# A two-layer triangle kernel: masks on the finished operands, and centring moved to VectorE

## The reference

```python
# layer 0 ("z")
z_norm = layer_norm(z)                         # over the 64 channels
a = (z_norm @ W_ap + b_ap) * sigmoid(z_norm @ W_ag + b_ag) * mask
b = (z_norm @ W_bp + b_bp) * sigmoid(z_norm @ W_bg + b_bg) * mask
z = z + (einsum('bikc,bkjc->bijc', a, b) @ W_z + b_z)
# layer 1 ("x")
x = layernorm(z)
left, right = sigmoid(x @ left1) * (x @ left2), sigmoid(x @ right1) * (x @ right2)
p = layernorm(einsum('nsre,nkre->nske', left, right))
out = z + einsum('nrse,ez->nsrz', p, out_w) * sigmoid(x @ gate)
```

## Time and profile before

| | us |
|---|---|
| median of 3 runs (lowest, highest) | 1227.56 (1223.94, 1231.35) |
| profiled execution | 1227.42 |
| its span | 1225.6 |
| PE, DVE, ACT, POOL busy | 900.5, 807.3, 583.7, 690.2 |
| POOL's pow x192 | 377.3 |
| POOL's mask of the gate x128 | 182.6 |

### The profile page before, as it was taken

One profiled execution on the slowest core, in us unless ns is written; L12 is line 12 of the kernel. 1 busy time (PEld: TensorE's weight loads), 2 busy tenths in 40 slices (PEclk: granted clock), 3 DMA queues, 4 the chain that ended last, 5 costly groups with the idle time before them and its releaser, 6 DMA issues.

```text
span 1225.6 us, 26377 instructions
## 1 busy us (share of the span) xinstructions
PE 900.5 (73%) x9820; PEld 849.1 (69%) x9820; DVE 807.3 (66%) x1883; ACT 583.7 (48%) x834; POOL 690.2 (56%) x441
## 2 busy tenths in 40 slices
PE   1546555467867689676967888888998999956965
PEld 1445454467867579665955888888898999946854
DVE  4888898945658851888167347662597299089097
ACT  1566666653935443455334445553454355333333
POOL 2576777766658851888045213331486188178097
PEclk9876667787988989999988899999999999989989
DMA  2334357776876733665766425676486288866156
GB/s 71 110 106 130 110 146 233 225 237 237 293 218 200 211 103 100 190 196 175 245 210 182 137 78 175 204 260 243 127 305 205 81 293 285 260 219 224 44 190 206
DMA packets 173238, 228.72 MB, mean 187 GB/s; under 512 B 11064, under 2 KB 109624, under 8 KB 171064
## 3 DMA queue, kind: packets, MB, share of 16 engines
q1 hardware_dynamic: 173112, 227.04, 59.4%
HBM read 134.73 MB, written 92.27 MB: 185 GB/s over the span
## 4 chain that ended last, share of the span: by engine, by line
PE 28%; DVE 26%; POOL 19%; issue 17%; ACT 4%; DMA 3%; SPq 2%; DVEq 0%; POOLq 0%; ACTq 0%
PE bank L918 18%; POOL rstd L511 13%; DVE stats L762 7%; DVE xc L795 6%; POOL sig L504 5%; DVE lhs L745 3%; PE ps_w L948 3%; PE bank L902 2%; DVE xc L787 2%; PE bank L903 2%; DVE var L770 2%; POOL xc L523 2%; DMA chunk<-xt 1%; DVE rhs L745 1%; PE ps_x L959 1%
## 5 line engine op out<-in xcount | busy, mean ns | idle before, releaser
L511 POOL TENSOR_TENSOR rstd<-var,minus_half 128x8 f32<-128x8 f32 x192 | 377.3, 1966 | 375.1 <-DVE var L770 375.0
L918 PE MATMUL bank<-rhs,lhs 128*128 128x128 f32 x2048 | 245.6, 283 | 15.5 <-DVE rhs L745 9.0
L504 POOL TENSOR_TENSOR sig<-sig,masks 128x512 f32<-128x512 f32 x128 | 182.6, 1433 | 128.4 <-ACT sig L569 127.5
L569 ACT ACTIVATE sig<-bank 128x512 f32<-128x512 f32 x256 | 153.1, 598 | 212.0 <-PE bank L903 202.0
L918 PEld LDWEIGHTS bank<-rhs,lhs 128*128 128x128 f32 x2048 | 241.0, 198 | 16.5 <-DVE rhs L745 9.5
L959 PE MATMUL ps_x<-ident_b,split 128*128 128x128 bf16 x1024 | 101.1, 257 | 142.9 <-DVE split L802 142.8
L795 DVE TENSOR_TENSOR xc<-xc,rstd 128x504 f32<-128x504 f32 (+1 forms) x192 | 161.1, 839 | 62.3 <-POOL xc L523 35.0
L902 PE MATMUL bank<-w_lhs,chunk 128*128 128x128 bf16 x1024 | 157.1, 242 | 51.7 <-DVE lhs L745 37.9
L902 PE MATMUL bank<-w_rhs,chunk 128*128 128x128 bf16 x1024 | 158.7, 245 | 40.4 <-DVE rhs L745 29.6
L959 PEld LDWEIGHTS ps_x<-ident_b,split 128*128 128x128 bf16 x1024 | 78.0, 116 | 158.5 <-DVE split L802 134.6
L948 PE MATMUL ps_w<-w_out,opair 128*128 128x128 f32 x1024 | 152.0, 296 | 39.1 <-DVE split L809 35.4
(11 more groups left out here) (83 smaller groups left out, 1348.7 us busy)
## 6 DMA issues: line engine op xcount, KB each, us to landing
xt<-xt SPq DMA_DIRECT2D x96, 512.0 KB, 4.4
chunk<-xt SPq DMA_DIRECT2D x80, 512.0 KB, 4.4
xin<-in_x_dram SPq DMA_DIRECT2D x128, 256.0 KB, 3.0
x<-xin SPq DMA_DIRECT2D x64, 256.0 KB, 3.7
xin<-x SPq DMA_DIRECT2D x64, 256.0 KB, 3.9
out_dram<-xin SPq DMA_DIRECT2D x64, 256.0 KB, 3.2
spill<-lhs SPq DMA_DIRECT2D x8, 1024.0 KB, 6.4
chunk<-xcol SPq DMA_DIRECT2D x16, 512.0 KB, 4.0
```

The lines of the kernel that those rows point to most:

```text
L504: g.tensor_tensor(sig[:, s], sig[:, s], table[:, other, first:first + COLS].unsqueeze(1).broadcast_to([P, C, COLS]), ALU.mult).then_inc(ma ...
L511: g.tensor_tensor(rstd[:, m % 2], var[:, m % 2], minus_half[:, :], ALU.pow).then_inc(rooted, 1)
L569: a.activation(sig[:, s], v[:, 0:C, :], ACT.Sigmoid).then_inc(gated, 1)
L918: last = mm(bank[:, n], operand["lhs"][:, kh, c, :], operand["rhs"][:, kh, c, :], start=kh == 0, stop=kh == HALVES - 1)
```

## The change

There are four edits, made together.

1. **Masks.** `mask_gate` goes: `make` waits for `gates` directly. Instead, finished operands are multiplied in place. POOL does 48 operations of 4 channels (128x512): one a tick from tick 22, two a tick from tick 54 (`mask_operand`). DVE does 24 of 8 channels (`mask_group`), eight at the start of each of the contractions 0 (128x1024), 1 and 2 (128x2048). PE waits for all 48 before contraction 0, and for each group of DVE's before that group. SP's first spills wait for POOL's masks, the next for DVE's.
2. **Centring.** DVE does all of it, except every other step of 52 to 63. Before, POOL also had every other step of the third `x` pass, all of the fourth, and every other one of the first two `p` passes.
3. **Order in a tick.** The first pass's halves run 5 ticks behind their step (53 ticks then), and a single half counts as a "second" half, whose gate and make come in the next tick. `z` steps are centred in their own tick, and `high` comes one tick earlier. In `x` steps `normalise`, `low`, `turn_x`, `xt_out` and the store come one tick later.
4. **Order on DVE**: `variance` directly behind `statistics`; `scale` ahead of `centre`.

```diff
-    lag = 6
-    for t in range(54):
+    lag = 5
+    for t in range(53):
         tick(t if t < 52 else None, [t - lag] if t >= lag else [])
+def first_half(t):
+    return halves_at(t)[0] if len(halves_at(t)) == 2 else None
+def second_half(t):
+    return halves_at(t)[-1] if halves_at(t) else None
+POOL_MASKS = 3 * C // 4
+MASK_FIRST, MASK_TWO = 22, 54
+def pool_masks_at(t):
+    if MASK_FIRST <= t < MASK_TWO:
+        return [t - MASK_FIRST]
+    if MASK_TWO <= t < MASK_TWO + C // 8:
+        return [2 * C // 4 + 2 * (t - MASK_TWO), 2 * C // 4 + 2 * (t - MASK_TWO) + 1]
+    return []
 def centre_on_pool(m):
-    kind = step(m)[0]
-    quadrant = m // STEPS
-    if kind == "z":
-        return m >= 52 and m % 2 == 0
-    if kind == "x":
-        return quadrant == 7 or (quadrant == 6 and m % 2 == 0)
-    return quadrant < 10 and m % 2 == 0
+    return SIG_STEPS[0] <= m < SIG_STEPS[1] and m % 2 == 0
+SIG_STEPS = (52, 64)
...
             def spill(layer, kh, part):
-                sp.wait_ge(made, after(2 * ((NEEDS[0] if layer == 0 else NEEDS[4])
-                                            - (0 if kh else CHUNKS // (2 if layer == 0 else 1))) - 1))
+                if layer == 0:
+                    if kh == 0:
+                        sp.wait_ge(masked_p, 2 * C // 4 + C // 16 * (part + 1))
+                    else:
+                        sp.wait_ge(masked_v, 2 * (part + 1))
...
+            def mask_operand(n):
+                kh, c = n // (C // 4) % 2, 4 * (n % (C // 4))
+                op, table = ("rhs", mask_kj) if n < 2 * C // 4 else ("lhs", mask_ki)
+                if c == 0:
+                    pool.wait_ge(made, after(CHUNKS * (n // (C // 4) + 1) - 1))
+                part = operand[op][:, kh, c:c + 4, :]
+                g.tensor_tensor(part, part, table[:, kh, 0:P].unsqueeze(1).broadcast_to([P, 4, P]),
+                                ALU.mult).then_inc(masked_p, 1)
...
+            def mask_group(q, group):
+                op, low_kh, high_kh = VECTOR_MASKS[q]
+                table, half = (mask_ki, P * (q == 1)) if op == "lhs" else (mask_kj, P)
+                dve.wait_ge(made, after(2 * NEEDS[q] - 1))
+                part = operand[op][:, low_kh:high_kh, CG * group:CG * (group + 1), :]
+                v.tensor_tensor(part, part, table[:, low_kh:high_kh, half:half + P].unsqueeze(2).broadcast_to(
+                    [P, high_kh - low_kh, CG, P]), ALU.mult).then_inc(masked_v, 1)
...
             def contract(q, u):
...
                 if part == 0:
+                    if q == 0:
+                        pe.wait_ge(masked_p, POOL_MASKS)
+                    if q in VECTOR_MASKS:
+                        pe.wait_ge(masked_v, GROUPS_C * q + u // 2 + 1)
...
         @block.scalar
...
             for t in range(T_END):
-                before, now = halves_at(t - 1), halves_at(t)
-                if len(before) == 2:
-                    gates(before[1])
+                if second_half(t - 1) is not None:
+                    gates(second_half(t - 1))
...
+                s = step_at(t - 1)
+                if s is not None and s < X_BASE:
+                    high(s)
                 s = step_at(t - 2)
-                if s is not None and s < P_BASE:
-                    high(s)
...
+                if first_half(t) is not None:
+                    gates(first_half(t))
...
         @block.vector
...
+                if unit and second_half(t - 1) is not None:
+                    make(second_half(t - 1))
+                if unit and unit[0] in VECTOR_MASKS and unit[1] < GROUPS_C:
+                    mask_group(unit[0], unit[1])
+                for s in (due, begin):
+                    if s is not None:
+                        statistics(s)
+                        variance(s)
+                if not unit and second_half(t - 1) is not None:
+                    make(second_half(t - 1))
...
```

More of the change, by code:

```diff
@@ L494, in _ @@
                             base=0, pattern=[[-1, P]], channel_multiplier=1).then_inc(idents, 1)
[L496 to L501, removed]
-                    pool.wait_ge(ready, 1)
[L503 to L506, removed]
+            def mask_operand(n):
+                kh, c = n // (C // 4) % 2, 4 * (n % (C // 4))
+                op, table = ("rhs", mask_kj) if n < 2 * C // 4 else ("lhs", mask_ki)
+                if n == 0:
+                    pool.wait_ge(ready, 1)
+                if c == 0:
[3 more added lines that the diff above has]
+                                ALU.mult).then_inc(masked_p, 1)
             def root(m):
@@ L549, in _ @@
                     add_residual(s)
-                if now and now[0] < 8 * CHUNKS:
-                    mask_gate(now[0])
+                for n in pool_masks_at(t):
+                    mask_operand(n)
         @block.scalar
@@ L817, in _ @@
             for t in range(T_END):
-                before, now = halves_at(t - 1), halves_at(t)
                 start, ago = step_at(t), step_at(t - 1)
-                if ago is not None and X_BASE <= ago < P_BASE:
-                    statistics(ago)
+                unit = TICKS[t][2]
+                due = ago if ago is not None and X_BASE <= ago < P_BASE else None
                 if start is not None and not X_BASE <= start < P_BASE:
-                    statistics(start)
-                if len(before) == 2:
-                    make(before[1])
@@ L826, in _ @@
[L826 to L831 removed]
+                    begin = start
+                else:
+                    begin = None
+                if unit and second_half(t - 1) is not None:
+                    make(second_half(t - 1))
@@ new lines, in _ @@
+                if unit and unit[0] in VECTOR_MASKS and unit[1] < GROUPS_C:
[6 more added lines that the diff above has]
+                    make(second_half(t - 1))
+                s = step_at(t - 3)
+                if s is not None and X_BASE <= s < P_BASE:
+                    low(s)
@@ L842, in _ @@
-                if now:
-                    make(now[0])
-                if ago is not None and centre_on_pool(ago):
-                    normalise(ago)
+                if first_half(t) is not None:
+                    make(first_half(t))
                 if ago is not None and ago >= P_BASE and ago % 2 == 0:
@@ L976, in _ @@
             for t in range(T_END):
-                now = halves_at(t)
-                start, s2 = step_at(t), step_at(t - 2)
+                start = step_at(t)
+                due = start if start is not None and X_BASE <= start < P_BASE else None
+                late = step_at(t - 2) if step_at(t - 2) is not None and step_at(t - 2) >= P_BASE else None
                 unit = TICKS[t][2]
-                first = bool(now) and t > 0 and TICKS[t - 1][2] is not None
+                first = first_half(t) is not None and t > 0 and TICKS[t - 1][2] is not None
                 if unit:
```

114 lines of the change are left out of this document (59 added, 55 removed).

## The result

The changed kernel took **1269.64 us** (median of 4 runs, 1266.82 to 1272.16); the kernel before 1225.89 beside it (1223.94 to 1231.35). The ratio is 1.0349 [1.0306, 1.0392]: slower by 3.5%. The prediction was 1259 and slower. The profiled execution took 1270.9, its span is 1269.1, its mean granted clock 0.88. In the experiments one execution of `e6_masks_ahead` (2714.88 us) and one of `e7_centring_alone` (1272.33 us) was disturbed; the ratios leave it out, the medians count it.

What follows compares the result with a forecast made beforehand. No engine bound the whole span; a loop through DVE, ACT and POOL set the first pass. Terms 47 + 13 - 3 + 9 + 5 - 19 - 17 - 1 - 8 + 6 = +32 on 1227.4 gave 1259 us, range 1226 to 1288.

Steps and rivals of the forecast that it cites:

- First pass: First pass: ticks lengthen through a closed wait loop, and POOL's masks hold low from tick 22; +60 us together.
- The ring: First pass: normalise, high, two copies, gate, make, low, centre wait in turn each tick; 5.50 us instead of 4.5, +47.
- The mask's hold: First pass from tick 22: POOL's operand mask delays DVE's low by 0.45 on 30 ticks; +13 us (0 to 32).
- Eight ticks and contraction 0: Ticks of two halves lose the gate's mask, -3; first contraction waits for POOL's last masks, PE 8 us late, +9.
- what is late next is SP's ring ... I take 5.3: Middle passes: SP's loads wait for store landings, so ticks take 5.3 us; -19 and -17.
- if the middle ticks are under 4.8: Middle passes: the prediction's own sign of being wrong, ticks below 4.8 us where it took 5.3.
- Rival (d): Middle passes: masks were not the limit, pow and DVE contention alone keep ticks at 6.5; 1295 us, chance 0.05.
- Pass without halves: x pass at 614.2: already runs on SP's loop of stores and loads, so little gain; -1 us (to -8).
- Pass at 714.2: x pass with two ticks per step: DVE's own centring replaces the wait for POOL's; -8 us (-4 to -12).
- Tail: Tail passes 0 and 1: 16 centrings return to a nearly full DVE, +6 us (0 to +10); passes 2 and 3: 0.
- Rival (a): Middle passes give everything back, DVE-bound at 4.7, masks not in low's way; 1226 us, no change, chance 0.09.
- rival (b): First pass: the wait loop does not close, a tick costs about 3.9; 1171 us, chance 0.06.

Runs made afterwards that it cites:

- e6_masks_ahead: Changed kernel with ACT's copies ahead of high (first pass), scale behind centre (tail), and POOL's masks from tick 54 ahead of pow and centring: 1166.17 us.
- e7_centring_alone: Kernel before with only the new centring rule (DVE does all but every other step of 52 to 63), old order: 1255.78 us.
- e1: Changed kernel with ACT's two copies issued ahead of high in the first pass, so the gate follows high directly: 1203.80 us.
- e2: Changed kernel with POOL's 32 first-pass masks cut to 1 channel instead of 4: 1261.24 us.
- e8: Kernel before, its own order and centring, with only the masks moved to finished operands (48 on POOL, 24 on DVE): 1147.27 us.
- e4: Changed kernel with scale put back behind centre on DVE in the tail passes, all centring staying on DVE: 1240.25 us.
- e9: Kernel before with masks on finished operands and the changed x steps (DVE centres, normalise and all behind it one tick later): 1101.48 us.

## Why the prediction was right, and where it was off

**First pass: right, in mechanism and size.** The ring closes (e1), 5.59 a tick against 5.50 predicted, and `make` waits 2.00 for the gate. The mask's hold was put at 0.45 on 30 ticks, 13 us; the makes behind tick 22 are 5.86 apart, 0.27 more than ahead of it, and e2 measures 8. That the term as a whole came out so near, +62 against +60, is in part luck: the two errors have opposite signs. That `make` is never held came true too: the trace has 676 to 693 ns for all 256 makes, next to masks and away from them.

**Eight ticks and contraction 0: right.** -3 as predicted; PE 8.9 late against 8, statistics 14.6 behind the last `make` against 13, +12 against +9. DVE's 16 masks of 2,048 elements ahead of and in contractions 1 and 2 took 2.28 to 2.29 each against 2.4. The Trainium skill's 2,293 ns for an fp32 tensor_tensor of that size (VectorE: DVE Perf Modes, the perf-mode tier table) is the better number; the trace agrees with it.

**Middle passes: the step that failed is "what is late next is SP's ring ... I take 5.3".** The tick is 4.70, the sum of DVE's operations that the prediction had worked out as 4.6 and then set aside; by its own sign ("if the middle ticks are under 4.8") this part of it is wrong. It had taken the landing time of stores from before (4.6) as given; in the faster pass it is 4.0, and 4.0 + 0.7 of issues is no longer above DVE's sum. SP does wait for landings there, 25.7 us in 410 to 490, but in its own slack: no wait of DVE's in that stretch ends with a load. Why the landings were shorter is not shown. The masks' 2.3 ahead of each contraction counted in, the two passes and contractions 1 and 2 gained 17 more than the terms gave. Rival (d), that pow alone keeps the old tick, is out; part of it was true of e8, where pow is the next wait.

**Pass without halves: mis-sized.** It was said to run on SP's ring already, read off one interval between stores (3.86), which would be 62 us for 16 steps. It took 68.4 with a centring of POOL's in every other step. -8 instead of -1; e7 shows it apart, with -6 from the centring alone.

**Pass at 714.2: right**, -6 against -8, within its bounds.

**Tail: mis-sized, by the largest error of all.** +31 in the first two passes instead of +6, and +5 in the third and fourth instead of 0. What was counted was right: the added centrings cost 7 (e4's first two passes against before; in e7, in the old order, 3.4 and 5.7). What was put at nothing is `scale`, which edit 4 puts ahead of `centre`, and so POOL's addition, which `scale` releases: the prediction never asked what stands beside what once the order has moved. e4 measures it at 24 in the first two passes and 5 in the other two.

So the sum was closer (11 us low) than its terms, and that is luck. Against the terms, 26 us of gain (the middle passes with their contractions, the pass without halves, contractions 3 and 4) and 37 us of loss (tail 30, contraction 0, the first pass and the pass at 714.2 the rest) were both missing. Rival (a) described the middle passes rightly and was wrong in that the mask would not hold `low` (it cost 8) and nothing else would be lost; rival (b), that the ring does not close, is excluded by e1.

## What to carry to other kernels

When a sequence is re-ordered on one engine, walk each ring again that leaves it and comes back: here one hand-over moved behind two unrelated copies cost 66 us, in a kernel in which no engine was the bound. Then ask for every pair of VectorE and GpSimd operations with all operands in SBUF which will start first in the new order; an addition that began 0.07 us ahead cost 24 us. And make parts of a change alone before judging the whole: moving the masks was worth 77 us, and moving centring with `normalise` 27, in a change that lost 44.

## What the runs showed of the hardware that was not expected

**Who comes first matters more than how long both take.** A POOL operation on two 128x512 operands in SBUF that starts 0.06 to 0.07 ahead of a DVE operation with two SBUF inputs makes that one take 1.75 instead of 0.68. When DVE is ahead (by 0.16 in e4), POOL's takes 1.57 to 1.66 instead of 1.26 and that operation of DVE's takes its usual 0.68. But the delayed POOL operation can still hold what follows on DVE: in e4 the copy 1.04 behind it took 1.18 instead of 0.68, and in e1 a mask that took 1.57 held `normalise`, which took 1.75. The copy, which has one SBUF input, is held from the start in the same way: 1.76 when the addition begins 0.08 ahead. It is what the Trainium skill says of the shared port pair (SBUF — State Buffer, "SBUF: two separate sides"), that whichever starts first has it for the whole instruction and the other blocks. The trace agrees, with 1.07 and 0.31 to 0.40 as the price on either side. Pow behaves otherwise: DVE's operations beside it were not stretched. Pow itself was. In the traces of the kernel before, of the changed one, of e4 and of e8 nearly all of its rows took 1.63 to 1.70 when pow began while DVE was idle or busy with an operation that reads PSUM, and 1.9 to 2.6 when it began during one of DVE's with two SBUF inputs (centring, `low` or a mask).

**A landing time is no constant.** The same 256 KB store took 4.6 in a pass with ticks of 6.5 and a DMA share of 0.64, and 4.0 in one with ticks of 4.7 and a share of 0.81: shorter where the traffic was denser.

**TensorE's clock** was granted at 0.58 in the first pass, where PE was busy 122.9 of 272.9 us; it was 0.67 before (115.6 of 210.7) and 0.93 in e9 (78.2 of 159.2). The lower clock goes with the longer pass here and is not its cause: DVE's waits in the pass all end with ACT's gate, and moving two copies on ACT (e1) took the time away.
